# Bias of the experts in three bfloat16 parts, a shorter choice of experts, and the weighted sum shared between TensorE and VectorE

## The chip, the cores and the metric

The kernel runs on one core of a Trainium2 chip. The metric is the device time of one execution in microseconds. TensorE (PE in the profile, PEld for its weight loads) multiplies matrices, VectorE (DVE) and ScalarE (ACT) work element by element, GpSimd (POOL) does the same and issues gathers, and SyncE (SP) issues plain DMAs.

## The reference

The reference is a chain of layers over `x` (4 images, 128 channels, 32 x 32 pixels, so 4096 tokens of 128). The change touches the last one only: a graph attention over 524288 edges gives every token 16 numbers (4 heads x 4 experts), they choose two of four experts, and the experts' outputs are added to the token with their weights.

```python
agg = jax.ops.segment_sum(msg, dst, num_segments=M).reshape(M, HEADS * NUM_EXPERTS) + b_gat
scores = _layernorm(agg, ln_gamma, ln_beta).reshape(M, HEADS, NUM_EXPERTS).mean(1)
topk_s, topk_i = jax.lax.top_k(scores, TOP_K)
w = jax.nn.softmax(topk_s, axis=-1)
for ei in range(NUM_EXPERTS):
    g = jnp.where(topk_i == ei, w, 0.0).sum(-1)
    hh = jax.nn.gelu(x @ W1[ei] + b1[ei], approximate=False)
    out = out + g[..., None] * (hh @ W2[ei] + b2[ei])
```

## The kernel before

The program is a row of stages. Inside a stage each engine has its own instruction list, written out by hand, and the lists are tied by semaphores; between stages all engines meet. Everything that the change touches lies in the last two stages.

**take_in_slots** (from about 2306 to 2511 us) does two things side by side. TensorE and ScalarE make the outputs of all four experts for all tokens: `Experts.multiply` walks 16 runs (4 images x 4 experts) in 32 halves of 512 tokens. A *round* of TensorE is: the hidden layer of one half (L2763, two float32 matmuls of 512 columns, which the profile counts as four), then the output of a half two rounds older: the bias `x2_b`, spread over the tokens by a matmul with one row of ones (L2774, one float32 matmul, counted as two), and eight matmuls of 128 columns (L2779, counted as 16). ScalarE (`Experts.bend`) takes the hidden layer through the GELU into a ring of three slots (L2811) and copies the outputs to `k.y` (L2799). The hidden layer has four PSUM banks, two halves deep.

Beside that GpSimd issues 128 gathers of edge slots (L3208) in four bands of 32. For each band ScalarE packs the rows (`pack`, L3218), VectorE works out maxima and exponents' arguments, ScalarE takes the exponentials (L3223, L3224), and VectorE sums. In ScalarE's list these pieces stand at fixed places between the halves: a band is packed after half 8, 15, 22 and 29 (`TO_PACK`), its exponentials follow one half later (`TO_BEND`), and after those of the second band ScalarE also waits for VectorE's `starting` (L3380). VectorE's list ends with the fourth band and two copies.

**choose_experts** (from 2514.8 us to the end) is first a chain on VectorE in which `link` makes each instruction wait for the one before. It merges the two sums of the attention, divides, normalises over the 16 numbers, averages over the heads into `s` (four scores for each token) and ranks the four scores pair by pair into `rank`. After a softmax the weights are turned by small matmuls (L3526) so that each lies in the partition of its token, and copied to `gates` (L3495). TensorE has meanwhile turned the tokens to channel-major (L3519) and ScalarE has stored them in place of the token-major ones (L3550).

Then comes the weighted sum, in 8 groups of 512 tokens. For each group VectorE makes 16 diagonal matrices (L3508, four in an instruction), TensorE multiplies the experts' outputs by them (L3533, 16 float32 matmuls of 128 columns, counted as 32), and VectorE adds the tokens (L3500). `diagonal` holds two groups. SyncE stores each group with one DMA (L3542).

## Time and profile before

| | |
|---|---|
| median of 3 runs | 2576.82 us (2575.9 to 2578.19) |
| the profiled execution's own time | 2575.91 us |
| its span, first to last instruction | 2574.1 us |
| mean granted TensorE clock | 0.828 |
| busy: PE, DVE, ACT, POOL | 1915.4, 1592.9, 1024.6, 723.4 us |
| last instruction of VectorE starts | 2571.00 us |

A row of the profile names the engine, the line of the kernel, the operation, `out<-in` by the program's names, and its count; in brackets stands how long the engine was idle before it and what ended that. The granted clock is a share of 2.4 GHz: 0.5 is the level of 1.2 GHz. The busy shares are means over the whole program; the last 270 us, a tenth of it, are what counts here.

### The profile page before, as it was taken

To read this page: it belongs to the slowest core of one execution; us is meant where nothing else is said; L and a number is where in the kernel's file an instruction comes from. 1 tells how busy PE (TensorE), PEld (TensorE's weight loads), DVE (VectorE), ACT (ScalarE), POOL (GpSimd) and SP (SyncE) were. 2 spreads that over 40 slices of the span, in tenths; PEclk is the share of its full clock that TensorE was granted. 3 is DMA by queue.
4 is the path that set the end of the run, shared out by engine and by line. 5 is a ranking of instruction groups with operands and counts; after the bars stand their busy time and mean duration, and the time that the engine had idled before them with its cause. 6 is when DMAs were issued, how large, how long until landed. Compare 5 with 4: busy or idle time off the path is not lost. (4 is left out here: it accounts for less than half of the span.)

```text
span 2574.1 us, 26674 instructions
## 1 busy us (share of the span) xinstructions
PE 1915.4 (74%) x8906; PEld 866.5 (34%) x8906; DVE 1592.9 (62%) x3660; ACT 1024.6 (40%) x1662; POOL 723.4 (28%) x693
## 2 busy tenths in 40 slices
PE   1594786787589566599978889887887887338595
PEld 1121321322233134456654333222322222124355
DVE  3477768768677775547667666566566563115567
ACT  0242142224304116445511544765765665224251
POOL 2300620440171041034450211233233123127730
PEclk7696887789689777789955998998998997659797
DMA  3300300300030000021020010110110100014100
GB/s 97 90 3 25 90 0 19 80 17 19 10 87 1 23 3 0 1 97 20 16 68 15 27 28 15 38 41 15 39 41 15 28 3 4 12 59 52 10 5 34
DMA packets 55807, 80.26 MB, mean 31 GB/s; under 512 B 17217, under 2 KB 28983, under 8 KB 55424
## 3 DMA queue, kind: packets, MB, share of 16 engines
q1 hardware_dynamic: 45158, 69.14, 9.0%
q10 hardware_dynamic: 6426, 7.99, 1.4%
q0 software_dynamic: 4096, 1.58, 1.3%
q8 instruction: 62, 1.02, 0.2%
q14 instruction: 65, 0.53, 0.1%
HBM read 50.13 MB, written 24.68 MB: 29 GB/s over the span
## 5 line engine op out<-in xcount | busy, mean ns | idle before, releaser
L2492 DVE TENSOR_REDUCE f_half_max<-f_ring 128x1 f32<-128x512 f32 x512 | 339.1, 686 | 286.7 <-PE f_ring L2156 284.3
L2375 ACT ACTIVATE f_probs<-f_ST 128x512 f32<-128x512 f32 x512 | 294.6, 597 | 262.6 <-PE f_ST L2183 259.0
L2156 PE MATMUL f_ring<-f_stacks 96*128 96x512 bf16 x512 | 215.3, 422 | 46.1 <-DVE f_half_max L2492 39.9
L772 DVE TENSOR_REDUCE att_half_max<-att_ring 128x1 f32<-128x512 f32 x256 | 161.2, 684 | 101.1 <-PE att_ring L659 92.2
L2183 PE MATMUL f_ST<-f_stacks 99*128 99x512 bf16 x512 | 207.1, 410 | 11.8 <-ACT f_probs L2375 11.8
L755 ACT ACTIVATE att_probs<-att_ST 128x1024 f32<-128x1024 f32 x128 | 129.3, 1023 | 155.9 <-PE att_ST L684 155.7
L2202 PE MATMUL f_O<-f_probs,f_v_ext 128*32 128x512 f32 x1024 | 157.5, 691 | 0.1
L3208 POOL DMA_INDIRECT ti_row<-features,slot_from x128 | 127.0, 992 | 56.4 <-issue 56.4
L659 PE MATMUL att_ring<-stacks 96*128 96x512 bf16 x256 | 104.5, 473 | 47.3 <-DMA stacks<-parts_dram 25.6
L684 PE MATMUL att_ST<-stacks 96*128 96x512 bf16 (+1 forms) x512 | 137.7, 398 | 0.0
L1242 DVE TENSOR_TENSOR loc_weighed<-loc_wide,l_pad 128x512 f32<-128x512 f32 x200 | 124.8, 684 | 19.9 <-PE loc_wide L1196 15.3
L702 PE MATMUL att_O<-att_probs,v_ext 128*64 128x512 f32 x512 | 130.5, 635 | 6.7 <-DVE att_den L791 6.7
L2156 PEld LDWEIGHTS f_ring<-f_stacks 96*128 96x128 bf16 x512 | 50.8, 99 | 249.5 <-DVE f_half_max L2492 168.3
L1739 ACT ACTIVATE bm_h<-bm_ps,bn 128x512 f32<-128x512 f32 x128 | 99.5, 777 | 78.2 <-PE bm_ps L1706 72.9
L1762 POOL TENSOR_TENSOR bm_h<-bm_h,bm_mix 128x512 f32<-128x512 f32 x64 | 82.0, 1303 | 159.6 <-ACT bm_h L1739 88.5
L1224 POOL TENSOR_TENSOR loc_partial<-loc_partial,loc_weighed 128x512 f32<-128x512 f32 x88 | 110.0, 1271 | 15.3 <-DVE loc_weighed L1242 11.8
L1053 POOL MEMSET loc_padded<- 104x1296 f32 x4 | 4.7, 1177 | 387.3 <-POOLq L43 387.3
L1202 PE MATMUL loc_acc<-loc_weighed,turned 128*128 128x512 f32 x208 | 111.2, 619 | 0.0
L2763 PE MATMUL gm_ps<-xn_cm,x 128*128 128x512 f32 x128 | 65.9, 643 | 44.8 <-ACT turned L2811 35.0
L1019 PE MATMUL loc_ps<-loc_prod,place 128*32 128x512 f32 (+1 forms) x208 | 56.8, 713 | 31.2 <-DVE loc_prod L1081 31.2
L2352 ACT CAST f_stacks<-f_ring 3x512 bf16<-3x512 f32 x64 | 36.9, 577 | 97.7 <-PE f_ring L2168 97.2
L684 PEld LDWEIGHTS att_ST<-stacks 96*128 96x128 bf16 (+1 forms) x512 | 49.4, 102 | 75.5 <-issue 17.5
(589 smaller groups left out, 3698.1 us busy)
## 6 DMA issues: line engine op xcount, KB each, us to landing
f_stacks<-f_parts SPq DMA_DIRECT2D x192, 64.0 KB, 2.2
parts_dram<-l_parts SPq DMA_DIRECT2D x8, 768.0 KB, 3.6
stacks<-parts_dram SPq DMA_DIRECT2D x24, 256.0 KB, 9.4
stacks<-parts_dram ACTq DMA_DIRECT2D x24, 256.0 KB, 10.5
f_parts<-f_parts SPq DMA_DIRECT2D x8, 768.0 KB, 3.4
es_raw<-L_ffn_edge_index SPq DMA_DIRECT2D x8, 512.0 KB, 4.1
bm_mix<-mix SPq DMA_DIRECT2D x8, 512.0 KB, 8.7
xn_cm<-x SPq DMA_DIRECT2D x1, 2048.0 KB
```

The lines of the kernel that those rows point to most:

```text
L684: last = nc.tensor.matmul(ST[:, s % 2, n * BANK:(n + 1) * BANK], k.stacks[0:rows, 1, per * h + j, m * P:(m + 1) * P], k.stacks[0:rows, 0, ...
L702: last = nc.tensor.matmul(O[at:at + width, :], k.v_ext[:, m, h, :], probs[:, s % probs_ring, n * BANK:(n + 1) * BANK], start=(m == 0), sto ...
L755: nc.scalar.activation(probs[:, s % probs_ring, :], ST[:, s % 2, :], ACT.Exp).then_inc(probs_ready, 1)
L772: nc.vector.tensor_reduce(half_max[:, h % 2, t, n:n + 1], ring[:, i % RING], AX.X, ALU.max, negate=True).then_inc(reduced, 1)
L1202: nc.tensor.matmul(acc[:, n], w_out, weighed[:, (i - LAG) % RING], start=(j == 0), stop=False).then_inc(summed, 1)
L1242: nc.vector.tensor_tensor(o_, a, v, ALU.mult).then_inc(weighed_ready, 1)
L2156: nc.tensor.matmul(ring[:, i % RING], f.stacks[0:STACK, 0, at, t * P:(t + 1) * P], f.stacks[0:STACK, 1, at, n * BANK:(n + 1) * BANK], star ...
L2183: nc.tensor.matmul(ST[:, i % HALVES], f.stacks[0:STACK + 3, 1, h % HEADS, m * P:(m + 1) * P], f.stacks[0:STACK + 3, 0, h % HEADS, n * BANK ...
L2202: last = nc.tensor.matmul(O[at:at + 32, :], f.v_ext[:, h // HEADS % 2, m, h % HEADS, :], f.probs[:, s % PROBS, n * BANK:(n + 1) * BANK], s ...
L2375: nc.scalar.activation(f.probs[:, s % PROBS, n * BANK:(n + 1) * BANK], ST[:, i % HALVES], ACT.Exp).then_inc(probs_ready, 1)
L2492: nc.vector.tensor_reduce(f.half_max[:, h % 2, t, n:n + 1], ring[:, i % RING], AX.X, ALU.max, negate=True).then_inc(reduced, 1)
L3208: self.nc.gpsimd.indirect_dma_start(self.row[:, j, :], None, self.k.features, bass.IndirectOffsetOnAxis(ap=self.k.slot_from[:, j:j + 1], a ...
```

## The change

The bias of the experts' output is split by VectorE into three bfloat16 parts whose sum is the float32 value (`split_bias`, at the head of VectorE's list in take_in_slots), and added by three bfloat16 matmuls with a row of bfloat16 ones. In choose_experts the attention's result keeps the layout [expert, head, token] in which it arrives, the mean over heads is taken before the row's scale is known (scale and offset parameters are divided by four by GpSimd), and the ranks are made for all pairs of one distance at a time. In the weighted sum TensorE keeps the even groups; for the odd groups VectorE adds weight times output to the token-major tokens, 16 instructions a group, TensorE turns the result and ScalarE copies it out. ScalarE makes the diagonals of the even groups, one matrix in an instruction; `diagonal` now holds all four groups. The first turning of the tokens is done for the even groups only.

```diff
             bank = take(2 * x + u)
-            nc.tensor.matmul(bank.rearrange("p (t n) -> p t n", n=P), k.ones_row[:],
-                             k.x2_b[0:1, e, :].unsqueeze(1).broadcast_to([1, 4, P]), start=True, stop=False)
+            if x == 0 and u == 0:
+                pe.wait_ge(parted, 6)
+            for part in range(3):
+                nc.tensor.matmul(bank.rearrange("p (t n) -> p t n", n=P), k.ones_b[:],
+                                 k.x2_parts[0:1, part, e, :].unsqueeze(1).broadcast_to([1, 4, P]), start=(part == 0),
+                                 stop=False)
             pe.wait_ge(hidden_off, 4 * x + 2 * (u + 1))
...
+        link = linker(dve, parted)
+        dve.wait_ge(k.late, 48)
+        link(nc.vector.tensor_copy(k.ones_b[:], k.ones_row[:]))
+        link(nc.vector.tensor_copy(k.x2_parts[:, 0], k.x2_b[:]))
+        link(nc.vector.tensor_tensor(k.x2_rest[:], k.x2_b[:], k.x2_parts[:, 0], ALU.subtract))
+        link(nc.vector.tensor_copy(k.x2_parts[:, 1], k.x2_rest[:]))
+        link(nc.vector.tensor_tensor(k.x2_rest[:], k.x2_rest[:], k.x2_parts[:, 1], ALU.subtract))
+        nc.vector.tensor_copy(k.x2_parts[:, 2], k.x2_rest[:]).then_inc(parted, 1)
...
+        diagonal = sb("ch_diagonal", [P, B, 4, E2, P])
...
-            for v in range(GE):
-                out = agg[:].rearrange("p t (h v) -> p v h t", v=GE)[:, v]
-                link(nc.vector.tensor_tensor(out, e.num[:, v], e.den[:], ALU.mult))
...
-            link(nc.vector.tensor_tensor(agg[:], agg[:], param(0), ALU.add))
-            link(nc.vector.tensor_reduce(st[:, 0], agg[:], AX.X, ALU.add))
-            link(nc.vector.tensor_scalar(st[:, 0], st[:, 0], 1.0 / 16, None, ALU.mult))
-            link(nc.vector.tensor_tensor(agg[:], agg[:], wide(st[:, 0]), ALU.subtract))
+            agg = e.num
+            link(nc.vector.tensor_tensor(agg[:], agg[:], e.den[:].unsqueeze(1).broadcast_to(whole), ALU.mult))
...
+            link(nc.vector.tensor_tensor(agg[:], agg[:], param(k.gat[:, 0]), ALU.add))
+            link(nc.vector.tensor_reduce(st[:, 0], agg[:].rearrange("p v h t -> p t (v h)"), AX.X, ALU.add))
+            link(nc.vector.scalar_tensor_tensor(rows(agg), over_units(st[:, 0]), -1.0 / 16, rows(agg), ALU.mult, ALU.add))
             link(nc.vector.tensor_tensor(sq[:], agg[:], agg[:], ALU.mult))
-            nc.vector.tensor_reduce(st[:, 1], sq[:], AX.X, ALU.add).then_inc(final, 1)
+            nc.vector.tensor_reduce(st[:, 1], sq[:].rearrange("p v h t -> p t (v h)"), AX.X, ALU.add).then_inc(final, 1)
+            dve.wait_ge(prepared, 8)
+            link(nc.vector.tensor_tensor(scaled[:], agg[:], param(quarter[:, 0]), ALU.mult))
+            link(nc.vector.tensor_reduce(s[:], scaled[:].rearrange("p v h t -> p v t h"), AX.X, ALU.add))
             dve.wait_ge(rooted, 1)
             link(nc.vector.reciprocal(st[:, 1], st[:, 1]))
-            link(nc.vector.tensor_tensor(agg[:], agg[:], wide(st[:, 1]), ALU.mult))
-            link(nc.vector.tensor_tensor(agg[:], agg[:], param(1), ALU.mult))
-            link(nc.vector.tensor_tensor(agg[:], agg[:], param(2), ALU.add))
-
-            link(nc.vector.tensor_reduce(s[:].rearrange("p v t -> p t v"), agg[:].rearrange("p t (h v) -> p t v h", v=GE),
-                                         AX.X, ALU.add))
-            link(nc.vector.tensor_scalar(s[:], s[:], 1.0 / GH, None, ALU.mult))
...
-                link(nc.vector.memset(rank[:, i], float(GE - 1 - i)))
-            for i in range(GE):
-                for j in range(i + 1, GE):
-                    link(nc.vector.tensor_tensor(st[:, 2], s[:, i], s[:, j], ALU.is_ge))
-                    link(nc.vector.tensor_tensor(rank[:, j], rank[:, j], st[:, 2], ALU.add))
-                    link(nc.vector.tensor_tensor(rank[:, i], rank[:, i], st[:, 2], ALU.subtract))
...
+            link(nc.vector.tensor_tensor(s[:], s[:], over_experts(st[:, 1]), ALU.mult))
+            link(nc.vector.tensor_tensor(s[:], s[:], beta[:].unsqueeze(2).broadcast_to([P, GE, MT]), ALU.add))
+
+            for d in range(1, GE):
+                n = GE - d
+                link(nc.vector.tensor_tensor(beats[:, 0:n], s[:, 0:n], s[:, d:GE], ALU.is_ge))
+                link(nc.vector.tensor_tensor(rank[:, d:GE], rank[:, d:GE], beats[:, 0:n], ALU.add))
+                link(nc.vector.tensor_tensor(rank[:, 0:n], rank[:, 0:n], beats[:, 0:n], ALU.subtract))
...
-            dve.wait_ge(carried, GROUPS)
-            for i in range(GROUPS):
-                if i >= 2:
-                    dve.wait_ge(mixed, i - 1)
-                for t in range(4):
-                    gate = gates[:, :, 4 * i + t].unsqueeze(2).broadcast_to([P, GE, P])
-                    nc.vector.tensor_tensor(diagonal[:, i % 2, t], k.ident[:].unsqueeze(1).broadcast_to([P, GE, P]), gate,
-                                            ALU.mult).then_inc(spread, 1)
-                if i >= 2:
-                    add(i - 2)
-            for i in range(GROUPS - 2, GROUPS):
-                add(i)
+            nc.vector.tensor_copy(gates[:].rearrange("p v t -> p (v t)"), ps[:, GROUPS - 1, 0:GE * MT]).then_inc(gated, 1)
+            dve.wait_ge(gated, 1)
+            done = 0
+            for i in range(1, GROUPS, 2):
+                for v in range(E2):
+                    for t in range(4):
+                        if v >= 1:
+                            dve.wait_ge(added, done - 3)
+                        x = tokens(i)[:, t]
+                        nc.vector.scalar_tensor_tensor(x, k.y[:, 4 * i + t, v], gates[:, v, 4 * i + t:4 * i + t + 1], x,
+                                                       ALU.mult, ALU.add).then_inc(added, 1)
+                        done += 1
+                dve.wait_ge(mixed, (i + 1) // 2)
+                nc.vector.tensor_tensor(result(i - 1), ps[:, i - 1], tokens(i - 1).rearrange("p t n -> p (t n)"),
+                                        ALU.add).then_inc(summed_by_dve, 1)
...
+            nc.gpsimd.tensor_scalar(quarter[:, 0], k.gat[:, 1], 1.0 / GH, None, ALU.mult).then_inc(prepared, 1)
...
+            for i in range(GE):
+                nc.gpsimd.memset(rank[:, i], float(GE - 1 - i)).then_inc(prepared, 1)
+            pool.wait_ge(prepared, 7)
+            nc.gpsimd.tensor_tensor(beta[:], halves[:, 0], halves[:, 1], ALU.add).then_inc(prepared, 1)
...
-            for i in range(GROUPS):
+            pe.wait_ge(carried, B)
+            for i in range(0, GROUPS, 2):
                 for t in range(4):
-                    pe.wait_ge(spread, 4 * i + t + 1)
+                    pe.wait_ge(spread, E2 * (2 * i + t + 1))
                     for v in range(E2):
-                        last = nc.tensor.matmul(ps[:, i, t * P:(t + 1) * P], k.y[:, 4 * i + t, v, :], diagonal[:, i % 2, t, v],
+                        last = nc.tensor.matmul(ps[:, i, t * P:(t + 1) * P], k.y[:, 4 * i + t, v, :], diagonal[:, i // 2, t, v],
                                                 start=(t == 0 and v == 0), stop=(t == 3 and v == E2 - 1))
                 last.then_inc(mixed, 1)
+                pe.wait_ge(added, 4 * E2 * (i // 2 + 1))
+                for t in range(4):
+                    last = nc.tensor.transpose(ps[:, i + 1, t * P:(t + 1) * P], tokens(i + 1)[:, t, :], k.ident[:])
+                last.then_inc(tokens_turned, 1)
...
+            act.wait_ge(gated, 1)
+
+            def carry_off(i):
+                act.wait_ge(tokens_turned, i // 2 + 1)
+                nc.scalar.copy(result(i), ps[:, i]).then_inc(summed_by_act, 1)
+
+            for i in range(0, GROUPS, 2):
+                for t in range(4):
+                    for v in range(E2):
+                        nc.scalar.activation(diagonal[:, i // 2, t, v], k.ident[:], ACT.Identity,
+                                             scale=gates[:, v, 4 * i + t:4 * i + t + 1]).then_inc(spread, 1)
+                if i >= 4:
+                    carry_off(i - 3)
+            for i in range(GROUPS - 3, GROUPS, 2):
+                carry_off(i)
```

VectorE's list in choose_experts, from the first product to the scores, before the change (`ch_agg` is the attention's result, `gat` the parameters, `ch_st` sums over 16 numbers, `ch_s` the scores):

```order
L3452 RECIPROCAL own_den<-own_den 128x128
L3455 TENSOR_TENSOR ch_agg<-own_num,own_den 128x4x32 x4
L3463 TENSOR_TENSOR ch_agg<-ch_agg,gat 128x512
L3464 TENSOR_REDUCE ch_st<-ch_agg 128x32
L3465 TENSOR_SCALAR ch_st<-ch_st 128x32
L3466 TENSOR_TENSOR ch_agg<-ch_agg,ch_st 128x512
L3467 TENSOR_TENSOR ch_sq<-ch_agg 128x512
L3468 TENSOR_REDUCE ch_st<-ch_sq 128x32
L3470 RECIPROCAL ch_st<-ch_st 128x32
L3471 TENSOR_TENSOR ch_agg<-ch_agg,ch_st 128x512
L3472 TENSOR_TENSOR ch_agg<-ch_agg,gat 128x512
L3473 TENSOR_TENSOR ch_agg<-ch_agg,gat 128x512
```

The same piece now, with `own_num` in place of `ch_agg`:

```order
L3479 RECIPROCAL own_den<-own_den 128x128
L3481 TENSOR_TENSOR own_num<-own_num,own_den 128x512
L3492 TENSOR_TENSOR own_num<-own_num,gat 128x512
L3493 TENSOR_REDUCE ch_st<-own_num 128x32
L3494 SCALAR_TENSOR_TENSOR own_num<-ch_st,own_num 128x512
L3495 TENSOR_TENSOR ch_sq<-own_num 128x512
L3496 TENSOR_REDUCE ch_st<-ch_sq 128x32
L3498 TENSOR_TENSOR ch_scaled<-own_num,ch_quarter 128x512
L3499 TENSOR_REDUCE ch_s<-ch_scaled 128x128
L3501 RECIPROCAL ch_st<-ch_st 128x32
```

The four divisions are one instruction and the scaling of the sums is folded into the subtraction; of the three wide products and additions behind the reciprocal one is left, and it stands ahead of it with the sum over heads. (Line numbers of these rows are those of the changed kernel.)

ScalarE's list in choose_experts before (token copies, square root, exponential, end of stage):

```order
L3550 COPY t_tm<-ch_ps 128x512 x8
L3552 ACT_TABLE_LOAD
L3552 ACTIVATE ch_st<-ch_st,eps 128x32
L3554 ACT_TABLE_LOAD
L3554 ACTIVATE ch_s<-ch_s 128x128
```

And now, with the diagonals and the copies of the odd groups:

```order
L3591 COPY t_tm<-ch_ps 128x512 x4
L3593 ACT_TABLE_LOAD
L3593 ACTIVATE ch_st<-ch_st,eps 128x32
L3595 ACT_TABLE_LOAD
L3595 ACTIVATE ch_s<-ch_s 128x128
L3605 ACTIVATE ch_diagonal<-ident,ch_gates 128x128 x48
L3600 COPY xn_cm<-ch_ps 128x512
L3605 ACTIVATE ch_diagonal<-ident,ch_gates 128x128 x16
L3600 COPY xn_cm<-ch_ps 128x512 x3
```

The 64 diagonals stand behind the exponential; the copies of groups 3, 5 and 7 stand behind the last of them.

VectorE's list behind the weights' copy, before:

```order
L3495 COPY ch_gates<-ch_ps 128x128
L3508 TENSOR_TENSOR ch_diagonal<-ident,ch_gates 128x512 x12
L3500 TENSOR_TENSOR xn_cm<-ch_ps,t_tm 128x512
L3508 TENSOR_TENSOR ch_diagonal<-ident,ch_gates 128x512 x4
L3500 TENSOR_TENSOR xn_cm<-ch_ps,t_tm 128x512
```

And now:

```order
L3523 COPY ch_gates<-ch_ps 128x128
L3532 SCALAR_TENSOR_TENSOR t_tm<-experts_y,ch_gates,t_tm 128x128 x16
L3536 TENSOR_TENSOR xn_cm<-ch_ps,t_tm 128x512
L3532 SCALAR_TENSOR_TENSOR t_tm<-experts_y,ch_gates,t_tm 128x128 x16
L3536 TENSOR_TENSOR xn_cm<-ch_ps,t_tm 128x512
```

The diagonals left VectorE; 16 weighted additions stand ahead of each addition of an even group, four times over. TensorE's list alternates accordingly: 16 matmuls of an even group, then four transposes of the odd group behind it.

## Rows read from the trace of the kernel before

**Rows 1.** The chain that ended last, in order of time: start us, duration us, engine, tile, line.
```profile
2520.63 0.39 DVE ch_agg L3455
...
2531.01 0.20 DVE ch_st L3483
...
2535.07 0.24 DVE ch_rank L3486
...
2537.53 0.30 DVE ch_s L3493
...
2539.40 0.30 DVE ch_gates L3495
...
2540.47 30.50 PE ch_ps L3533 x256
...
2571.00 0.69 DVE xn_cm L3500
```

**Rows 2.** Timeline of TensorE, 2429 to 2442 us; in brackets the idle time before and its releaser.
```profile
2429.27 3.78 PE L2763 MATMUL gm_ps<-xn_cm,x 128*128 128x512 f32 x4 [27.11 <-ACT turned L2811]
2432.98 2.07 PE L2774 MATMUL gm_ps<-x_b,ones_row 1*128 1x512 f32 x2
2434.98 3.54 PE L2779 MATMUL gm_ps<-x,turned 128*128 128x128 f32 x16
2438.36 1.88 PE L2763 MATMUL gm_ps<-xn_cm,x 128*128 128x512 f32 x4
2440.17 1.12 PE L2774 MATMUL gm_ps<-x_b,ones_row 1*128 1x512 f32 x2
2441.22 2.05 PE L2779 MATMUL gm_ps<-x,turned 128*128 128x128 f32 x16
```

**Rows 3.** Timeline of ScalarE, then of VectorE, in the stage take_in_slots.
```profile
2391.22 2.10 ACT L3218 COPY ti_packed<-ti_row 128x768 f32<-128x768 f32 x1 [2.69 <-DMA ti_row<-features,slot_from]
...
2426.80 0.42 ACT L3380 ACTIVATE ts_n<-ts_n 128x256 f32<-128x256 f32 x1 [24.79 <-DVE ts_n L3404]
...
2453.29 2.10 ACT L3218 COPY ti_packed<-ti_row 128x768 f32<-128x768 f32 x1
...
2486.55 2.10 ACT L3218 COPY ti_packed<-ti_row 128x768 f32<-128x768 f32 x1
...
2511.21 0.23 DVE L3334 COPY slot_tile<-rf_tile 128x128 f32<-128x128 f32 x1
```

**Rows 4.** Timeline of TensorE at 1801.7 us, bfloat16 matmuls in line.
```profile
1801.70 0.38 PE L2183 MATMUL f_ST<-f_stacks 99*128 99x512 bf16 x1
1801.92 0.38 PE L2156 MATMUL f_ring<-f_stacks 96*128 96x512 bf16 x1
```

**Rows 5.** Timeline, start of take_in_slots: TensorE's first matmuls, VectorE's first instruction.
```profile
2307.81 7.40 PE L2763 MATMUL gm_ps<-xn_cm,x 128*128 128x512 f32 x12 [9.86 <-DMA x_b<-L_ffn_b]
...
2318.00 4.50 DVE L3313 MAX8 rf_eight<-rf_pool 128x8 f32<-128x4160 f32 x1 [33.09 <-DMA rf_pool<-left_codes]
```

**Rows 6.** Groups of VectorE instructions, shapes apart: count, busy us, mean ns, idle.
```profile
L3412 DVE SCALAR_TENSOR_TENSOR own_num<-ts_n,ts_last,own_num 128x32 f32<-128x32 f32 x16 | 4.0, 252 | 0.6
...
L3475 DVE TENSOR_REDUCE ch_s<-ch_agg 128x128 f32<-128x512 f32 x1 | 1.1, 1057 | 0.0
...
L3464 DVE TENSOR_REDUCE ch_st<-ch_agg 128x32 f32<-128x512 f32 x1 | 0.7, 686 | 0.0
```

**Rows 7.** Timeline rows of VectorE and ScalarE without waits between; groups of ScalarE.
```profile
2230.76 1.64 DVE L2395 BATCH_NORM_STATS2 f_moments_tail<-f_xn 128x6 f32<-128x128 f32 x8
...
1298.48 3.19 ACT L2237 ACTIVATE f_xn<-t_tm,f_norm_pre 128x128 f32<-128x128 f32 x8 [12.79 <-POOL f_norm_pre L2578]
...
L2375 ACT ACTIVATE f_probs<-f_ST 128x512 f32<-128x512 f32 x512 | 294.6, 597 | 262.6 <-PE f_ST L2183 259.0
...
L1739 ACT ACTIVATE bm_h<-bm_ps,bn 128x512 f32<-128x512 f32 x128 | 99.5, 777 | 78.2 <-PE bm_ps L1706 72.9
```

**Rows 8.** Stretches: length, busy of PE, PEld, DVE, ACT, POOL, PEclk, DMA share, GB/s.
```profile
2351.50:2354.20 2.70, 0.00 (x1) 0.00 (x0) 0.46 (x1) 2.66 (x3) 1.92 (x3) 1.00 0.09 9
```

More of the change, by code:

```diff
@@ L2751, in out_bank, with multiply @@
         return self.ps[:, self.HIDDEN + i % self.OUT]
-    def multiply(self, pe, hidden_ready, hidden_off, made, carried):
+    def multiply(self, pe, parted, hidden_ready, hidden_off, made, carried):
         nc, k = self.nc, self.k
@@ L3346, in take_in_slots @@
         (block, chained, fetched, starting, started, shifted, exped, packed, banded, pool_in, drawn, stored, spread,
-         hidden_ready, hidden_off, made, carried, *gathered) = c.enter_context(stage(
+         parted, hidden_ready, hidden_off, made, carried, *gathered) = c.enter_context(stage(
              nc, "chained", "fetched", "starting", "started", "shifted", "exped", "packed", "banded", "pool_in", "drawn",
-             "stored", "spread", "hidden_ready", "hidden_off", "made", "carried",
+             "stored", "spread", "parted", "hidden_ready", "hidden_off", "made", "carried",
              *(f"gathered_{g}" for g in range(BANDS)), pool_dma=True))
@@ L3353, in _ @@
         def _(pe):
-            experts.multiply(pe, hidden_ready, hidden_off, made, carried)
+            experts.multiply(pe, parted, hidden_ready, hidden_off, made, carried)
         @block.sync
@@ L3445, in _ @@
             nc.vector.tensor_tensor(both[:, 1], e.shift[:], both[:, 2], ALU.subtract).then_inc(final, 1)
+            whole = [P, GE, GH, MT]
             dve.wait_ge(exped, 1)
@@ L3448, in _ @@
                 link(nc.vector.tensor_tensor(den[:], den[:], part, ALU.mult))
-                link(nc.vector.tensor_tensor(num[:], num[:], part.unsqueeze(1).broadcast_to([P, GE, GH, MT]), ALU.mult))
+                link(nc.vector.tensor_tensor(num[:], num[:], part.unsqueeze(1).broadcast_to(whole), ALU.mult))
             link(nc.vector.scalar_tensor_tensor(e.den[:], e.den[:], 1e-16, k.den[:], ALU.add, ALU.add))
@@ L3464, in _, with rows, param @@
-            link(nc.vector.tensor_reduce(st[:, 0], agg[:], AX.X, ALU.add))
-            link(nc.vector.tensor_scalar(st[:, 0], st[:, 0], 1.0 / 16, None, ALU.mult))
-            link(nc.vector.tensor_tensor(agg[:], agg[:], wide(st[:, 0]), ALU.subtract))
+            agg = e.num
+            link(nc.vector.tensor_tensor(agg[:], agg[:], e.den[:].unsqueeze(1).broadcast_to(whole), ALU.mult))
+            def rows(x):
+                return x[:].rearrange("p v h t -> p (v h) t")
+            def param(a):
+                return by_heads(a).unsqueeze(3).broadcast_to(whole)
@@ L3475, in _, with over_experts @@
[L3475 to L3485 removed]
+            def over_experts(a):
+                return a.unsqueeze(1).broadcast_to([P, GE, MT])
@@ L3547, in _ @@
             nc.scalar.activation(both[:, 0:2], both[:, 0:2], ACT.Exp).then_inc(exped, 1)
-            for i in range(GROUPS):
-                act.wait_ge(turned, i + 1)
+            for i in range(0, GROUPS, 2):
+                act.wait_ge(turned, i // 2 + 1)
                 nc.scalar.copy(tokens(i).rearrange("p t n -> p (t n)"), ps[:, i]).then_inc(carried, 1)
@@ L3554, in _ @@
             nc.scalar.activation(s[:], s[:], ACT.Exp).then_inc(exped, 1)
+            act.wait_ge(gated, 1)
+            def carry_off(i):
+                act.wait_ge(tokens_turned, i // 2 + 1)
+                nc.scalar.copy(result(i), ps[:, i]).then_inc(summed_by_act, 1)
+            for i in range(0, GROUPS, 2):
+                for t in range(4):
[6 more added lines that the diff above has]
+                carry_off(i)
 class Edges:
```

52 lines of the change are left out of this document (30 added, 22 removed).

## The prediction

> **What bounds the kernel now.** I read the page's busy shares first and put them aside: they are means over the whole program, and the change touches only its last 270 us. The chain of waits comes next. It names what ends last, and in choose_experts it is one thread: VectorE alone, one linked instruction behind the other, from 2516 to 2538 us, then TensorE with the 256 counted matmuls of the weighted sum, 30.5 us, then one addition [rows 1]. The weights stand in `gates` at 2539.70 and the last addition ends at 2571.69, so this tail is 31.99 us. In it TensorE is the bound: 8 groups, the first 5.5 us and the other seven 3.57 us each (30.5 less 5.5, by seven).
>
> For take_in_slots the timeline says more than the chain, which stops at the stage's border. The stage ends with VectorE's last copy, 2511.21 + 0.23 [rows 3]. That copy stands at the end of the fourth band, which VectorE starts when ScalarE has packed it (2486.55 + 2.10) and then needs 22.8 us. ScalarE reaches that packing by its own list, half by half behind TensorE: 33.26 us after the third packing, which is seven rounds of 4.75. The third packing stands four rounds behind ScalarE's wait for VectorE, which ends at 2426.80 [rows 3]. The second packing, however, waited 2.69 us for the gathers [rows 3]: a faster TensorE reaches it earlier and waits longer. So of the 32 rounds only eleven lie on the path, the first of them at the lower clock: 9.09 us where the others take 4.75 [rows 2].
>
> **The bias as three bfloat16 matmuls.** At full clock the bias takes 1.05 us from its start to that of the next product (2440.17 to 2441.22), at the lower one 2.00 [rows 2]. Two float32 passes of 512 columns are all it has, so about 0.2 us of it is the handover to the next weights, which wait behind ScalarE's signal; that stays. A bfloat16 matmul of 512 columns with its own weight load follows another in 0.22 us [rows 4]. Three are 0.66, with the handover 0.86: 0.19 us less. At the lower clock I take twice the matmul time and 0.3 for the handover: 3 x 0.43 + 0.3 = 1.6, so 0.4 less. Ten times 0.19 and 0.4 make **2.3 us**. Bounds: should a weight load of one row not hide behind the short matmul (0.1 us each), the bias takes 1.16, and 1.1 to 1.5 us are lost instead; should the first round lose to the lower clock no more than the tail's first group did (5.5 instead of 3.57, so 1.9, where this round loses 4.3, 0.3 of it already counted), another 2.1 are gained. I take 2.3, since the rows of the matmul are of the very length.
>
> The split itself is hidden. VectorE was idle for 33 us until its first instruction of the stage at 2318.00, and TensorE has 7.4 us of hidden layers from 2307.81 before it asks for a bias [rows 5]. Six linked instructions of at most 0.69 us (the price of a 512-wide one [rows 6]) are 4.3. Without that cover they would cost just that.
>
> A round shorter by 0.19 uses up a cover. While ScalarE waits for VectorE between packing and exponentials, TensorE lives on four hidden banks; before, ScalarE had freed the first of them 0.7 us before TensorE wanted it, three rounds after the packing. Three times 0.19 is 0.57: still no stall, but it is close, and beyond 0.25 a round each further gain is given back.
>
> **The chain of the choice.** From 2520.63 to the first comparison at 2531.01 the old list takes 10.38 us [rows 1]. The new one has five 512-wide products, additions and squares at 0.69 and 0.03 for the link; three sums that read across the layout; one reciprocal, 0.38; two 128-wide instructions at 0.325 (the chain has one at 0.30 and its link [rows 1]). The sums are the unknown. The contiguous one took 0.686 us, the one that reads every fourth number 1.057 [rows 6]; the new ones read every 32nd. I take the dearer row, 1.08 with its link, being the only strided one. 5 x 0.73 + 3 x 1.08 + 0.38 + 0.65 = 7.9 us: 2.5 less. The memsets are gone to GpSimd, which has ten microseconds for eight small instructions before VectorE asks.
>
> Ranks: 18 steps of 32 columns took 4.06 us (2531.01 to 2535.07), 0.226 each [rows 1]. Nine steps of 96, 64 and 32 columns at 0.29, 0.26 and 0.226 are 2.3: 1.8 less. Together **4.2 us**; with contiguous prices 5.3, with sums a half dearer than the dear row 2.6.
>
> The Trainium skill, "SBUF — State Buffer" ("Door 1: The DMA port swizzle"), has a rule that speaks against this layout: the memory has lines of 16 bytes, and each access that enters a new line pays, so that four float32 are the free stride. By that rule both the old stride of four numbers and the new ones of 32 pay, and the dear row is the right one; it gives no size, and the trace agrees with its sign by 1.057 against 0.686 us. By a flat price per column the sum would be 5.3, by the rule with the row's size 4.2.
>
> **The weighted sum.** Count from the moment the weights are in `gates`. ScalarE makes 64 diagonals. Eight 128-wide ones with two operands by pointer took 3.19 us at 0.48 each, so one follows another in 0.387; two pointers make a 512-wide one dearer by 0.18 (0.777 against 0.597), one by 0.09 [rows 7]. With one pointer I take 0.297: 1.19 us for the four of a token tile, 4.75 a group. VectorE makes 64 weighted additions, each waiting only for the fourth before it. Eight unlinked 128-wide instructions took 1.64 us [rows 7], 0.195 apart; a pointer scalar makes a 32-wide one 0.252 [rows 6] where the plain ones of the ranks are 0.20 [rows 1], so 0.06 more, and one that reads two tensors is no cheaper: 0.27 apart, 4.4 us a group, and 0.7 for the addition of the even one. TensorE needs 3.57 a group, 1.9 more in the first, and some 0.45 for four transposes.
>
> Follow it: TensorE starts at 1.3 and ends group 0 at 6.8, where the old pace gives 5.5 + 1.3. VectorE, done with group 1 at 4.4, waits for it and adds until 7.5. Group 3 is weighted at 11.9, the addition ends at 12.6, group 5 at 17.0 and 17.7, group 7 at 22.1. TensorE meanwhile ends group 2 at 10.8, waits 1.1 us for VectorE, turns, ends group 4 at 15.9, waits 1.1, ends group 6 at 21.0, waits 1.1. After 22.1: the transposes, 22.5, and ScalarE's copy, 23.1. So VectorE is the new bound, with a period of 5.1 us for two groups instead of 7.15, and the tail is 23.1 us: 8.9 less. The last two DMAs now start almost together; I take 0.2 back. **8.7 us.** Bounds: additions 0.20 apart make TensorE and ScalarE the bound, last copy at 21.6; additions that don't overlap at all (0.385) put it at 28.6, and 3.4 are left.
>
> Sum: 2.3 + 4.2 + 8.7 = 15.2 us. Against the profiled execution's own 2575.91 that is 2560.7; the median lay 0.9 above it, so **2561.6 us**.
>
> **The rivals.** A difference under 0.2%, 5.2 us, can't be told from none here.
>
> *ScalarE becomes the bound.* A diagonal that pays the two-pointer pace, 0.387, makes the last of group 6 ready at 25.4 and the last copy 27.4: the tail gains 4.4, the whole 10.9, 2565.9 us. For it: 0.387 is the only measured pace of that shape. Against: the bias is a constant here. In old terms VectorE made four diagonals in 0.69 us. The Trainium skill, "ScalarE: Activation LUTs" ("Rules for kernel authors"), has multiplications go to VectorE for that reason; by it the move costs the tail what this rival says. Chance 0.10.
>
> *The clock falls back in the tail.* TensorE now waits 1.1 us between groups and starts later. If it stays at 1.2 GHz, a group takes 7.0 us, four with transposes end at 32.9, the copy at 33.5: the tail loses 1.5, 10.2 less than forecast, 2571.8 us. Against: TensorE sat idle throughout 2351.5 to 2354.2 us with the granted clock at 1.00 [rows 8]; after 27 us of idleness it had fallen [rows 2]. The Trainium skill, "TensorE: Matmul & The Clock Gate" (Part 1), agrees that activity releases a throttle that idleness brings back. Chance 0.07.
>
> *VectorE's additions are dear.* Not overlapped: 2567.1 us, chance 0.07, inside my range. The same mechanism decides on the other side: 64 additions and 4.7 us must fit into 32 + 6.3 us (what the other terms give). From 0.53 us each nothing is left, from 0.61 the kernel is slower by more than can be mistaken; at 0.65 the time is 2585 us. The place is VectorE's 16 additions in place on `t_tm`, each reading what the fourth before it wrote. No row of that width without GpSimd beside it is over 0.30, so 0.03.
>
> *The bias gains nothing*, because weight loads show: 2564.9 us, chance 0.10, inside.
>
> **How the numbers follow.** Likeliest, within 3 us of 2561.6: 0.60; the rivals 0.10, 0.07, 0.07, 0.03, 0.10; 0.03 for what I don't see. The range goes from 2555 (contiguous sums, cheap additions, an earlier clock: 15.2 + 1.1 + 1.5 + 2.1 gives 2557, and a run's spread) to 2569 (additions not overlapped and the bias without gain). Left out are the clock, the slow side and some of the unseen. Faster: all but a half of the clock's case and the slow one, 0.91; same 0.05; slower 0.04.
>
> **What would show it.** In the changed profile: the bias row 0.86 us ahead of the product; packings 4.56 us a round apart; VectorE's copies ending the stage 2.3 us earlier; strided sums at 1.0 to 1.1; 7.9 us from the first product to the first comparison; the additions in runs of 16 of about 4.4 us with idle of TensorE released by them; a granted clock near 1.0 over the tail behind its first group. It is wrong if TensorE waits for diagonals rather than additions, or if a pack waits for gathers.

## The result, and the profile after

The changed kernel took 2558.39 us in the median of 4 runs (2555.49 to 2560.33), the kernel before 2577.51 (2575.9 to 2581.12): ratio 0.9923, interval 0.9906 to 0.994. Forecast were 2561.6 us, between 2555 and 2569. A second series of both kernels gave 2562.33 against 2576.28 us, ratio 0.9945 (0.9932 to 0.9958).

The profiled execution took 2560.33 us, with a span of 2558.5: 15.6 less than the one before. It started the stage late, though: GpSimd's first gather was issued at 2308.26 us, 1.83 later than before (2306.43), with nothing changed ahead of it. From that mark to the end of the span the difference is 17.4 us, and this is the number to be explained. The stage take_in_slots after, in its timeline (ScalarE, TensorE, ScalarE, VectorE; to be read against [rows 2, 3]):

```profile
2393.69 2.10 ACT L3234 COPY ti_packed<-ti_row 128x768 f32<-128x768 f32 x1 [8.98 <-DMA ti_row<-features,slot_from]
...
2429.79 0.42 ACT L3396 ACTIVATE ts_n<-ts_n 128x256 f32<-128x256 f32 x1 [25.31 <-DVE ts_n L3421]
...
2432.26 3.78 PE L2763 MATMUL gm_ps<-xn_cm,x 128*128 128x512 f32 x4 [26.95 <-ACT turned L2827]
2435.97 1.03 PE L2777 MATMUL gm_ps<-x_parts,ones_b 1*128 1x512 bf16 x3
2436.93 2.05 PE L2783 MATMUL gm_ps<-x,turned 128*128 128x128 f32 x16
2438.82 1.88 PE L2763 MATMUL gm_ps<-xn_cm,x 128*128 128x512 f32 x4
2440.64 0.82 PE L2777 MATMUL gm_ps<-x_parts,ones_b 1*128 1x512 bf16 x3
2441.38 2.05 PE L2783 MATMUL gm_ps<-x,turned 128*128 128x128 f32 x16
...
2452.85 2.10 ACT L3234 COPY ti_packed<-ti_row 128x768 f32<-128x768 f32 x1
...
2484.27 2.10 ACT L3234 COPY ti_packed<-ti_row 128x768 f32<-128x768 f32 x1
...
2508.91 0.23 DVE L3350 COPY slot_tile<-rf_tile 128x128 f32<-128x128 f32 x1
```

The second packing now waits 8.98 us for the gathers, where it waited 2.69: what TensorE gained up to there is lost in this wait, as foretold. The gathers set the place of the packing: 85.43 us behind the first of them, before 84.79. From there ScalarE's exponential (2429.79) follows on VectorE's chain. Only behind it does a shorter round count. I call *the stretch* the time from this exponential to the start of VectorE's last copy: 84.41 us before (2426.80 to 2511.21), 79.12 now. The bias stands 0.74 us ahead of its product (2440.64 to 2441.38), and a round takes 4.45 us, 0.30 less. Eleven rounds at 0.30, less 0.27 that a packing costs again (shown below), give 3.0. The other 2.3 us are the first round, 6.56 us (2432.26 to 2438.82) where it took 9.09, under a higher mean granted clock (length of the round, busy PE, PEld, DVE, ACT, POOL, granted clock, DMA share, GB/s; before, then changed):

```profile
2429.27:2438.36 9.09, 9.09 (x23) 5.05 (x24) 5.61 (x19) 3.92 (x7) 6.96 (x8) 0.51 0.15 12
2432.26:2438.82 6.56, 6.56 (x23) 3.32 (x24) 5.59 (x19) 3.92 (x7) 4.82 (x6) 0.68 0.14 10
```

The stretch is 5.3 us shorter but begins 1.2 later behind the first gather (121.53 us, before 120.37). That distance lies between 120.4 and 121.5 us in all fourteen profiles, and the changed kernel profiled again had 120.73 (e12_changed_again), so most of the 1.2 us is scatter.

The chain that ended last, for choose_experts after (start, duration, engine, tile, line):

```profile
2518.23 0.70 DVE own_num L3481
...
2519.68 1.02 DVE ch_st L3493
...
2523.82 1.03 DVE ch_s L3499
...
2532.50 0.30 DVE ch_gates L3523
2532.82 1.29 ACT ch_diagonal L3605 x4
2534.25 6.02 PE ch_ps L3570 x32
2540.29 0.69 DVE xn_cm L3536
2540.98 4.20 DVE t_tm L3532 x16
2545.18 0.60 DVE xn_cm L3536
2545.78 4.20 DVE t_tm L3532 x16
2549.98 0.60 DVE xn_cm L3536
2550.58 3.94 DVE t_tm L3532 x15
2554.83 0.67 PE ch_ps L3575 x4
2555.53 0.59 ACT xn_cm L3600
```

In [rows 1] the end of this chain was one block of TensorE, 30.50 us. Now TensorE stands in it with its first group and four transposes, and behind the first group VectorE follows itself, 4.80 us for two groups. The tail, from the weights in `gates` (2532.79) to the last result (2556.12), is 23.33 us; it was 32.00. From the first wide product (2518.23) to the first comparison (2525.91) it is 7.68 us, the ranks take 2.33 (to 2528.24); they were 10.38 and 4.06.

How TensorE and ScalarE pass the tail (timeline):

```profile
2534.25 6.00 PE L3570 MATMUL ch_ps<-ch_diagonal,experts_y 128*128 128x128 f32 x32 [1.78 <-ACT ch_diagonal L3605]
...
2545.23 0.66 PE L3575 MATMUL ch_ps<-ident,t_tm 128*128 128x128 f32 x4 [0.97 <-DVE t_tm L3532]
2545.73 3.74 PE L3570 MATMUL ch_ps<-ch_diagonal,experts_y 128*128 128x128 f32 x32
2550.03 0.66 PE L3575 MATMUL ch_ps<-ident,t_tm 128*128 128x128 f32 x4 [0.57 <-DVE t_tm L3532]
...
2532.82 14.13 ACT L3605 ACTIVATE ch_diagonal<-ident,ch_gates 128x128 f32<-128x128 f32 x48 [3.28 <-DVE ch_gates L3523]
```

ScalarE makes 48 diagonals in 14.13 us, 0.294 apart, the 0.297 of the sum. TensorE's idle time ends on VectorE's additions (`t_tm` L3532) and never on a diagonal but the first.

### The profile page after: what moved, and what is told of

It is laid out like the page before. It is cut to its first block and busy times, and to the rows that moved or that the text cites. A ratio compares the mean times of both kernels' runs of the same rounds, so it can differ in the third digit from the quotient of the medians.

```text
span 2558.5 us, 26567 instructions
## 1 busy us (share of the span) xinstructions
PE 1900.4 (74%) x8810; PEld 847.6 (33%) x8810; DVE 1584.3 (62%) x3676; ACT 1044.0 (41%) x1726; POOL 727.9 (28%) x701
## 5 line engine op out<-in xcount | busy, mean ns | idle before, releaser
L2183 PE MATMUL f_ST<-f_stacks 99*128 99x512 bf16 x512 | 209.7, 415 | 11.8 <-ACT f_probs L2375 11.8
L1719 PEld LDWEIGHTS bm_ps<-mo,bm_h 128*128 128x128 f32 x512 | 65.9, 191 | 25.8 <-issue 24.6
```

The costliest lines, as they stand in the source:

```text
L2183: nc.tensor.matmul(ST[:, i % HALVES], f.stacks[0:STACK + 3, 1, h % HEADS, m * P:(m + 1) * P], f.stacks[0:STACK + 3, 0, h % HEADS, n * BANK ...
```

## The experiments

The totals scatter: the kernel before alone ran from 2565.31 to 2585.16 us in the 27 runs beside the first four kernels. I therefore read each effect from its own stretch of the trace, and give the ratio beside it.

**One part at a time.** e1_bias, e2_choice and e3_sum are the kernel before with one part of the change each, whose code is that of the diff above. e4_two_parts leaves the third part of the bias out of the sum:

```diff
-            for part in range(3):
+            for part in range(2):
```

> The kernel before with the bias in three bfloat16 parts and nothing else. In the changed kernel the stretch from ScalarE's exponential behind its wait for VectorE to VectorE's last copy of take_in_slots fell from 84.41 us (2426.80 to 2511.21) to 79.12 us. Theory: 3.0 us of this are ten rounds of 4.45 instead of 4.75 us, and the other 2.3 to 2.5 us are the first round, in which TensorE reached the upper clock after 4.7 us instead of after 9. If the shorter bias causes the early clock, this kernel's stretch is again about 79.1 us and the kernel is about 5.3 us faster than before. Rival (chance): the moment at which the clock comes back has nothing to do with the bias; then the first round is 9.1 - 0.3 us here or any value between 6.5 and 9, and the stretch 79 to 81.4 us. Rival (a stall): the time is as before, because the second packing waits longer for the gathers; then the stretch is shorter all the same but the stage's start to the second packing longer. The part of the stage up to the second packing should be set by GpSimd's gathers alone: packing about 85 us behind the first gather in every run.

> The kernel before with the new choice of experts (layout, mean before scale, ranks by distance) and the old bias and old weighted sum. Theory: only VectorE's chain is shorter: 7.7 us from the first wide product to the first comparison instead of 10.4, 2.3 us of ranks instead of 4.06; 4.4 us faster, about 2573. Rival: the weighted sum starts earlier on a TensorE that is at the lower clock longer and gives some of it back; then the 256 matmuls take more than 30.5 us.

> The kernel before with the new weighted sum alone (half of the groups by VectorE, diagonals by ScalarE). Theory: the tail from the weights in gates to the last result is 23.1 to 23.4 us instead of 31.99, VectorE being the bound with 4.8 us for two groups; 8.7 us faster, about 2569. Rival: ScalarE is the bound at 0.387 us a diagonal, tail 27.4 us, 4.4 us faster.

> The changed kernel with only the first two of the three bfloat16 parts added (the third is left out of the sum). Theory: the bias is a price per matmul, 0.22 us each, and a small handover of 0.08 us: the bias row to product distance falls from 0.74 to 0.52 us, the round from 4.45 to 4.23 us, and ten rounds are 2.2 us shorter; the stretch behind ScalarE's wait is about 77 us. Rival: the round is bound by ScalarE's signal and not by the bias matmuls; then the round stays 4.45 us. Rival: VectorE's packing chain, not TensorE, limits the rounds that follow a packing; then less than 2.2 us is gained, because TensorE stalls for a free hidden bank there.

Measured (us; the first round is from its hidden layer's start to that of the next):

| kernel | stretch | first round | product to comparison, ranks | tail | ratio to before |
|---|---|---|---|---|---|
| before | 84.41 | 9.09 | 10.38, 4.06 | 32.00 | |
| changed | 79.12 | 6.56 | 7.68, 2.33 | 23.33 | 0.9923 (0.9906 to 0.994) |
| e1_bias | 78.91 | 6.34 | 10.37, 4.06 | 32.21 | 0.999 (0.9979 to 1.0002) |
| e2_choice | 81.93 | 6.64 | 7.68, 2.33 | 32.78 | 0.9985 (0.9968 to 1.0001) |
| e3_sum | 85.88 | 9.29 | 10.37, 4.06 | 23.21 | 0.9969 (0.9956 to 0.9983) |
| e4_two_parts | 79.22 | 8.17 | 7.67, 2.34 | 23.49 | 0.9942 (0.9915 to 0.9969) |

Each part does in its own stretch what it does in the whole; what moves beside that is the clock. The choice is worth 2.70 + 1.73 = 4.4 us and the sum 8.7. The totals agree: against 2578.0 us, the median of the 27 runs, the three parts alone take 3.1, 4.1 and 7.9 us off, 15.2 together, though only the interval of e3_sum excludes 1. e2_choice's tail is 0.8 us longer than before, because TensorE's block spent more of itself at the lower clock. That this comes from the earlier start, as the rival has it, isn't shown: e5_awake below has the old choice and a tail of 32.71 us. The old tail simply lies between 32.0 and 32.8. The table also splits the bias. e2_choice has the old bias and a first round of 6.64 us; so an early return of the clock doesn't need the short bias, and against this kernel e1_bias gains 81.93 - 78.91 = 3.0 us: 0.30 in the first round, 0.30 in each of the ten others, less 0.27 at the packing. The other 2.3 us of the profiled execution belong to the clock, which comes back early or late in kernels of either kind. In e3_sum it comes back so late that the second round, too, is long, 6.02 us for 4.75. The gathers keep their pace in all profiles: the second packing stands 84.6 to 85.4 us behind the first gather.

e4_two_parts gives the price of one matmul: the bias stands 0.53 us ahead of its product (2462.28 to 2462.81), the round is 4.23. The stretch is 79.22 us all the same, not the 77 expected, because the clock came back late (first round 8.17) and because of a stall: between the third packing and the fourth, seven rounds apart, lie 30.56 us, not 29.61. Its timeline shows where 0.66 of the missing 0.95 went:

```profile
2462.28 0.60 PE L2777 MATMUL gm_ps<-x_parts,ones_b 1*128 1x512 bf16 x2
2462.81 2.05 PE L2783 MATMUL gm_ps<-x,turned 128*128 128x128 f32 x16
2464.69 1.88 PE L2763 MATMUL gm_ps<-xn_cm,x 128*128 128x512 f32 x4
...
2469.75 1.98 PE L2763 MATMUL gm_ps<-xn_cm,x 128*128 128x512 f32 x4 [0.66 <-ACT turned L2827]
```

TensorE waits for a hidden bank that ScalarE frees late behind its packing. With three parts the packings lie 31.42 us apart where seven rounds make 31.15, so 0.27 is lost there.

**The clock.** TensorE idles some 27 us ahead of that first round. e5_awake is the kernel before with work for it there, matmuls whose result nobody reads. e8_awake_both is the changed kernel with the same and with 9 such matmuls ahead of the tail, e10_steady the changed kernel with 30 and with 14 and one more ahead of the tail. The core of e5_awake, ahead of the hidden layer of half 18:

```diff
+            pe.wait_ge(carried, 13)
+            for _ in range(27):
+                nc.tensor.matmul(self.out_bank(16), k.x1[:, 0, 0:P], chunk(k.xn_cm[:, 0], 0), start=True, stop=True)
```

and in e10_steady, where the steps are places in VectorE's list:

```diff
+            for step, count in ((0, 5), (52, 3), (56, 3), (60, 3), (64, 4), (67, 5), (84, 7)):
+                if step:
+                    pe.wait_ge(chained, step)
+                for _ in range(count):
```

> The kernel before, in which TensorE does 27 float32 matmuls of 512 columns into an output bank that stands free (24.4 us at 0.905 us each) while it waits about 27 us for ScalarE in take_in_slots. So far the first round behind that wait took 9.09 (before), 6.64 (e2_choice), 9.29 (e3_sum) with the old bias, and the stretch behind the wait 84.4, 81.9 and 85.9 us. Theory: the whole loss of the first round is the lower clock of a TensorE that was idle; then the round is 4.75 us here, and the stretch 80.0 us (81.93 less the 1.9 that e2_choice's first round still lost). Rival: the first round's length is something else (an output bank, ScalarE's catching up after its wait); then it is 6.6 to 9.3 us again although the granted clock is 1.0. Rival: the 27 matmuls last longer than the wait and delay the rounds, so that the stretch is longer.

> The changed kernel with the 27 idle-time matmuls of e5_awake and, in choose_experts, 9 float32 matmuls of 512 columns behind the turning of the tokens, during VectorE's chain. Theory: the first round behind ScalarE's wait takes 4.45 us (it took 6.35 to 6.56 or 8.2 us), the stretch to VectorE's last copy about 77.1 us; in the tail the first group takes 4.75 us, as long as ScalarE needs for its 16 diagonals, instead of 6.0, VectorE waits 1.3 us less for it, and the tail is about 22.0 us instead of 23.3. Rival: the clock falls back between the 9 matmuls and the tail (they end some 4 us or more before the weights' matmuls), and the tail is 23.3 us as before.

> The changed kernel in which TensorE is kept busy without a long gap: in take_in_slots 30 float32 matmuls of 512 columns in seven lots, six of them released by steps of VectorE's chain, so that the last ends about when ScalarE frees the first bank; in choose_experts 14 behind the turning of the tokens and one between the weights' turning and the weighted sum. In e5_awake TensorE was idle for 7.4 us behind its 27 matmuls and the granted clock fell from 1.00 to 0.50 during that; in e8_awake_both 3.5 us, and it fell 1 us into the round. Theory: with gaps under 1 us it stays at 1.00, the first round takes 4.45 us, the stretch from ScalarE's exponential to VectorE's last copy 77.0 us in this run and in any other; in the tail the first group is bound by ScalarE's 16 diagonals (ends 5.7 us behind the weights instead of 7.5) and the tail is 21.5 us instead of 23.33. Rival: the clock falls in spite of it (then something else than idleness takes it away), and the first round stays at 6.4 to 8.2 us.

Measured: e5_awake's first round took 9.29 us and its second 6.01, its stretch 85.87 (ratio 0.9996, 0.9983 to 1.0008). TensorE began its wait earlier than in the profiles before, so 7.4 us were left open, and the stretches (length, busy of PE, PEld, DVE, ACT, POOL, granted clock, DMA share, GB/s) show the clock go in them:

```profile
2403.00:2422.00 19.00, 19.00 (x46) 8.50 (x45) 17.89 (x33) 0.00 (x0) 14.73 (x15) 1.00 0.12 9
2422.00:2424.00 2.00, 0.84 (x2) 0.01 (x1) 1.76 (x7) 0.00 (x0) 1.70 (x2) 1.00 0.17 9
2424.00:2426.00 2.00, 0.00 (x0) 0.00 (x0) 1.83 (x6) 0.00 (x0) 1.39 (x3) 0.74 0.16 10
2426.00:2430.00 4.00, 0.00 (x0) 0.00 (x0) 3.17 (x12) 2.24 (x3) 3.09 (x4) 0.50 0.19 10
2430.00:2440.00 10.00, 9.80 (x23) 5.59 (x24) 5.79 (x20) 4.39 (x9) 7.56 (x9) 0.50 0.11 10
```

So this run did not test what it was made for: busy for 23 us, TensorE lost the clock in the gap behind. In e8_awake_both the gap was 3.5 us; the clock was still 1.00 when the round began and fell within it, and the round took 7.79 us, the stretch 80.42 (77.1 expected). Its tail was 22.60 us, 0.6 more than forecast for it, since TensorE stood idle again for 6.8 us ahead of turning the weights. e10_steady left no gap over 0.75 us there:

```profile
2405.00:2430.00 25.00, 23.04 (x51) 9.00 (x50) 22.09 (x44) 1.18 (x2) 19.21 (x20) 1.00 0.13 9
2430.00:2435.00 5.00, 4.25 (x11) 1.66 (x10) 4.07 (x15) 2.58 (x4) 3.87 (x4) 1.00 0.18 10
2435.00:2440.00 5.00, 5.00 (x25) 2.97 (x26) 4.47 (x16) 4.06 (x8) 3.78 (x4) 1.00 0.14 10
```

Its first round took 4.55 us and its stretch 77.12 (77.0 expected); the tail took 21.89 us (21.5 expected), with the first group done in 4.57 instead of 6.00 us. Ratio 0.9928 (0.9911 to 0.9945). e8_awake_both and e10_steady differ in when TensorE gets this work, and little in how much: where the clock held, the first round took 4.55 us, 0.10 more than the rounds behind it, and where it fell, 7.79. So the lower clock behind idleness is the loss of the first round, all but 0.1 us.

**What bounds the tail.** All three are the changed kernel with an edit. In e6_linked the loops over tile and expert change places, so that the additions of experts 1 to 3 wait for the one right before them (wait for `done` instead of `done - 3`). The addition of expert 0, every fourth, waits for none: 12 of 16 are linked. In e7_reorder VectorE's list is 1, 3, add 0, 5, add 2, 7, add 4, add 6:

```diff
-                dve.wait_ge(mixed, (i + 1) // 2)
+                for j in {1: (), 3: (0,), 5: (2,), 7: (4, 6)}[i]:
+                    dve.wait_ge(mixed, j // 2 + 1)
```

and e9_pool is e7_reorder with the diagonals of group 6 made by four instructions of GpSimd instead of 16 of ScalarE.

> The changed kernel with the loops over tile and expert of VectorE's weighted additions exchanged, so that each addition waits for the one right before it instead of for the fourth before it. In the changed kernel 16 take 4.28 us, 0.262 apart. Theory: the spacing is bought by the order in which neighbours don't depend on one another; a linked one comes 0.33 us after another (the 128-wide linked ones of the chain: 0.325 apart), 16 take 5.2 us, and since VectorE is the bound the tail is 4 x 0.95 - 0.9 (the first 16 stand before TensorE's first group and are covered) = 2.8 us longer, about 26.2 us. Rival (my old bound): 0.385 apart, 16 in 6.2 us, tail 28.6. Rival: no dependence matters, 0.262 again.

> The changed kernel in which VectorE weights groups 1 and 3 before it adds the tokens of group 0 (then 5, 2, 7, 4, 6), so that it doesn't stand idle for the 3.17 us in which it waits for TensorE's first group. Theory: VectorE ends its 64 additions 3.2 us earlier, and ScalarE's 64 diagonals (0.297 us each, 19.05 us, and one copy) become the bound: the last diagonal is ready 19.6 us behind the weights, TensorE's last group 0.9 us later, the last result 0.7 behind that or with the turned group 1.5: tail 21.3 us instead of 23.33. Rival: the tail stays at 23.3 us, since TensorE's transposes wait in its own list for VectorE's order.

> e7_reorder with the 16 diagonals of the last even group made by GpSimd (four instructions of 128x512) instead of ScalarE, which then has 48. e7_reorder's tail took 21.60 us, with ScalarE's diagonals back to back until 19.2 us behind the weights and TensorE's last group stretched to 4.66 us by them. Theory: ScalarE was the bound; now TensorE is (5.8 us for the first group, 3.6 to 4.0 and 0.43 of turning for each further one), and the last result stands 20.2 us behind the weights. Rival: GpSimd's wide products (1.30 us for one of 128x512 in this program) hold up VectorE's additions, which then take more than 4.28 us for 16, and the tail is 22 us or longer.

Measured (one run, 2568.54 us): e6_linked's 16 additions take 5.79 us, 0.36 apart in the mean, and its tail 27.24 us (26.2 expected). The mean mixes two prices: a linked addition follows the one before after 0.387 us, an unlinked one after 0.27. The 0.33 I expected is neither. A linked addition with a pointer is dearer than a plain linked product, and costs the 0.385 of the prediction's bound. VectorE as bound is confirmed: three times 1.51 us came on top of 23.33, less the 0.6 by which TensorE's first group was ready earlier than in the changed kernel. e7_reorder's tail is 21.60 us (21.3 expected); ScalarE is the bound there, TensorE's last group being stretched to 4.66 us by the diagonals. The ratio, 0.9947 (0.993 to 0.9965), is no better than the changed kernel's: 1.7 us don't show in the total. e9_pool took ScalarE's load away and lost 1.1 us: 22.74. Its rows for VectorE and GpSimd:

```profile
2530.38 11.75 DVE L3532 SCALAR_TENSOR_TENSOR t_tm<-experts_y,ch_gates,t_tm 128x128 f32<-128x128 f32 x32
...
2530.43 4.21 POOL L3555 TENSOR_TENSOR ch_diagonal<-ident,ch_gates 128x512 f32<-128x512 f32 x4 [18.94 <-DVE ch_gates L3523]
```

The 32 additions took 8.49 us in e7_reorder; beside 4.21 us of GpSimd they took 3.26 us more. The first four came 1.05 to 1.16 us apart, one to each instruction of GpSimd, the others 0.262 again. The rival was right, the ratio 0.9947 again (0.993 to 0.9965).

**Together.** e11_all is e10_steady with e7_reorder's list, in which VectorE makes the last four diagonals; e12_changed_again is the changed kernel beside it.

> The changed kernel with e10_steady's idle-time matmuls, e7_reorder's order of VectorE's list, and the last four diagonals (tile 3 of group 6) made by VectorE in one instruction ahead of group 7's additions, so that ScalarE has 60. Theory: the parts add. The stretch in take_in_slots is 77.1 us as in e10_steady. In the tail ScalarE ends its 60 diagonals and one copy 18.4 us behind the weights, TensorE's last group 1 to 1.6 us later, the last result is there 20.4 us behind the weights (changed kernel 23.33, e7_reorder 21.60, e10_steady 21.89). Against the changed kernel of the same rounds that is 2.9 us in the tail and 1.8 us or more in the stage, depending on where that kernel's clock comes back: about 5 us less. Rival: the total doesn't move beyond its scatter, because that is made ahead of the two stages; then the intervals of both kernels overlap although both stretches are shorter. Rival: the diagonals by VectorE delay group 7 and the tail stays at 21.6 us.

> The changed kernel once more, as it is, beside e11_all. Theory: if the moment at which the clock comes back is chance, its stretch in take_in_slots lies anywhere from 78.9 to 81.4 us (79.12 in the first profile); the tail is again 23.3 us within 0.2, the chain of the choice 7.68 and 2.33 us. The ratio to the kernel before should be about 1 less (3.0 + 4.4 + 8.7) / 2577 = 0.9937, and not the 0.9923 of the first four runs.

Measured: e11_all 2557.36 us, ratio 0.9926 (0.9912 to 0.994); e12_changed_again 2562.33 us, 0.9945 (0.9932 to 0.9958). e11_all's stretch is 77.12 us and its tail 21.32, not 20.4: I had left out that tile 3 follows tile 2 on TensorE and that turning and copying (1.2 us) stand behind both. e12_changed_again: stretch 79.24, first round 6.67, choice 7.68 and 2.33, tail 23.36. The traces say 2.1 + 2.0 us less for e11_all; the medians say 5.0, and the intervals of the ratios overlap, so the total bears it out only weakly.

## Why the prediction was right

*Bias.* The mechanism held, the size didn't: 3.0 us instead of 2.3. The step that was off is the handover (from the end of the bias's matmuls to the start of the product) of 0.2 us, taken over from the float32 form. One matmul costs the 0.22 us of [rows 4] (0.74 less 0.53), so the handover is 0.74 - 3 x 0.22 = 0.08. The split was hidden as argued: it ran from 2309.75 to 2312.73 us, and TensorE asked for the bias later. The eleven rounds on the path were the right ones, and the second packing waits longer. The limit of 0.25 us a round was about right: at 0.30 a packing loses 0.27 us, at 0.52 it loses 0.95. By the letter one sign of being wrong came true, a pack that waits for gathers: the second one does, as it did before and as the prediction says elsewhere; the third and fourth do not. And VectorE's last copy stands 2.30 us earlier in the span (2508.91 against 2511.21), the very 2.3 forecast, but by luck: 5.3 us of shorter stretch, less 1.8 by which the stage started later and 1.2 by which the stretch began later in it.

*The clock of the first round.* The other 2.3 us of the stretch stood in the bounds (2.1), not in the sum. The first round took 9.1, 6.6 and 9.3 us with the old bias and a full idle wait, and between 6.2 and 8.5 in the seven profiles with the new one and the same wait. Whether the new bias makes the early return likelier stays open; three profiles against seven don't tell.

*Choice.* 4.4 us against 4.2. The sums that read across the layout took 1.01 us, near the dear row's 1.057 and far from the contiguous 0.686, so the price by the row was right. The dear row has 128 results and the contiguous one 32, so [rows 6] alone left open whether the results cost it; now a sum with 32 results takes 1.01 us and one with 128 takes 1.02, so it is the layout. A stride of 32 numbers costs about what a stride of 4 does, which agrees with the Trainium skill, "SBUF — State Buffer" ("Door 1: The DMA port swizzle"), in that each access to a new line of 16 bytes pays. Read as four float32 being a stride without cost, the same note isn't borne out, since the stride of four took 1.057 us against 0.686. Ranks took 2.33 us for 2.3.

*Weighted sum.* The mechanism is the one forecast, VectorE as the bound. Additions lie 0.262 us apart (0.27 forecast), diagonals 0.294 (0.297), the time for two groups is 4.8 us (5.1), and TensorE waits 0.97 and 0.57 us where 1.1 was said. The first group cost 6.0 us, not 5.5; behind it the granted clock was 1.00, over 2541 to 2556. That the tail took 23.33 us for 23.1 is partly luck: VectorE was through with its first addition of an even group 0.6 us later than forecast, made up 0.7 over the three pairs of groups that follow, and the turning and copying at the end took 0.3 more than forecast. The 0.2 us taken back for the last two DMAs rested on no row, and no run shows it: from the last result to the end of the span it was 2.41 us before and 2.38 after. It happens to stand in for the 0.2 that the tail was longer. ScalarE as bound is refuted by 48 diagonals in 14.13 us, dear additions by 16 in 4.28. The price of that last rival was right: linked additions do come 0.387 us apart (e6_linked); waiting for the fourth before is what avoids it.

*Total.* Stretches give 3.0 + 4.4 + 8.7 = 16.1 us for 15.2 forecast, the two series 19.1 and 14.0. In the profiled pair the 16.1 and the clock's 2.3, less the 1.2 of the later stretch, make 17.2 of the 17.4 us from the first gather on. The first median lies 3.2 us under the forecast, the second 0.7 over it.

## What to carry to other kernels

Before pricing a faster stage, find the wait that no speed-up removes (here 64 gathers at 1.25 us each) and count only the rounds behind it. Where work is shared between engines, go through the list of the one that becomes the bound: VectorE's 3.17 us of waiting for a group of a TensorE at the lower clock was worth 1.7 us, read from the tail, and a change of order removed it. An effect of a few us in a program that scatters by up to twenty is read from its own stretch in several traces; one trace credits a change with the clock's luck.

## What the runs showed of the hardware

A TensorE kept busy for 23 us had a granted clock of 0.50 again after a gap of 7.4 us (e5_awake), was caught with 1.00 at the end of one of 3.5 us and lost it in the next microsecond though busy (e8_awake_both), and kept it over gaps of up to 0.75 us (e10_steady). In choose_experts of e10_steady a gap of 2.6 us ahead of turning the weights took it away, at 2531.2 us, and it was back at 2534.6, ahead of the first group. Back at work behind some 27 us of idleness, it reached the upper level after 3.3 to 11.8 us, and differently in kernels with the same code in this stage: 8.9, 3.6 and 11.8 us in before, e2_choice and e3_sum, 3.3 to 8.4 with the new bias. The Trainium skill, "TensorE: Matmul & The Clock Gate" (Part 1), has the clock go with idleness and come back with work, with which these rows agree, save that in e8_awake_both it went only when work had begun again.

GpSimd's 4.21 us of wide products cost VectorE 3.26 us: while they ran, VectorE got one addition done for each of them instead of four (e9_pool). A weighted addition of 128 columns follows the one before it after 0.262 us when it doesn't wait for it, and after 0.387 when it does (e6_linked).
